# A mixture-of-experts kernel: row codes from one matrix product, two slots joined on TensorE instead of three, and the read-back mixed in after the last items

## The chip, the cores and the metric

The kernel runs on 1 core of one Trainium2 chip. The metric is the device time of one execution in microseconds (us); the kernel before takes 216.29 us (median of 3 runs, 215.59 to 216.37).

## The reference

```python
x = x + ffn(cond(x))                     # x: 32 x 32 tokens, 256 features, float32
def cond(x):                             # a linear layer with one low-rank adapter per batch
    H = einsum('btd,od->bto', x, W)
    return H + einsum('btr,bor->bto', einsum('btd,brd->btr', x, A[idx]), Bm[idx]) * scalings[idx]
def ffn(c):                              # 8 experts, hidden width 704, each token goes to two of them
    weights = softmax_integer(c @ w_gate.T)
    top_w, top_i = top_k(weights, 2); top_w = top_w / top_w.sum(-1)
    out = sum over experts e: combine[:, e] * ((silu(c @ w1[e].T) * (c @ w3[e].T)) @ w2[e].T)
```

## The kernel before

Every token is needed by two experts, so 2048 rows are sorted by expert and packed into 23 slots of 128 rows, each slot of one expert. The kernel first computes the conditioned rows (`c_rows`), the router logits and, on VectorE, each row's position (`pos`). GpSimd then sends rows to their slots in DRAM by indirect DMAs (`send`, two for each of 8 token tiles), and slots 1 to 3 are gathered directly from `cond_rows` (`gather`). For that the kernel needs the token of every slot row (`src_i`), which TensorE makes as a sum of one-hot products, and the row to which each result belongs (`dst_i`, `destinations`), from 24 more such products (`where_rows_belong`). Slot 0 is picked by a product of its own (L1122).

The main loop has 69 items, three for each slot (`s`, `j` = item `i` by 3). In item `i` TensorE does `gate_up(i)`, sometimes `turn_slot` (transposes of the next slot), `turn_hidden(i-1)` and `down(i-2)`. ScalarE does `silu(i)`, `slot_hi` and `hidden_hi(i-1)`; VectorE does `hidden(i)`, `slot_lo`, `hidden_lo(i-1)` and, at `j` = 1, the copy of the finished slot (`slot_out`). Every float32 operand is split into a high and a low part, the weights too: `expert_lo` on VectorE makes the low parts of experts 0 and 1, `low` on GpSimd those of the others. Weights come from the queue of SyncE (`raw_weights`).

The order on each engine is written out by hand and each engine works strictly in it; semaphores are the only ties (`pe.wait_ge(y_out, s)` holds the next slot's `down` until the copy of the last slot is made). The results of the first `SENT` slots go to DRAM by indirect DMAs (`scatter`), are read back in eight DMAs once all of them have landed, scaled (`scale_first`, ScalarE), mixed (`mix`, VectorE) and turned (`turn_sent`, TensorE). The results of the last `DIRECT` slots never leave the core: `join` multiplies them with one-hot matrices (`hot_out`, made by GpSimd, L556) into the four output banks `gu`, two products for each bank and slot. VectorE adds `x` to each bank (L970), and SyncE stores it.

## Time and profile before

| what | value |
|---|---|
| median of 3 runs | 216.29 us |
| the profiled execution | 216.09 us |
| its span in the profile | 214.0 us |
| TensorE busy | 198.9 us, 93% of the span |
| VectorE, ScalarE, GpSimd busy | 50%, 39%, 63% |

The profile shows one execution. Its span is 2.1 us shorter than the time of the same execution, for what lies around it. Times in the rows are us from the start of the span. PE is TensorE, PEld its weight loads, DVE VectorE, ACT ScalarE, POOL GpSimd and SPq the DMA queue of SyncE.

### The profile page before, as it was taken

What the parts mean: (1) busy time and instruction counts of PE and PEld (TensorE: products, weight loads), DVE (VectorE), ACT (ScalarE), POOL (GpSimd) and SP (SyncE); (2) the same over time, 40 slices, a digit from 0 to 9 for tenths busy, and PEclk for the clock granted to TensorE, in tenths of its full rate; (3) what the DMA queues carried; (4) which work ended last, traced back from release to release, by engine and by line L of the source; (5) the groups of instructions that cost most, each with busy time, mean ns of one, the idle gap of its engine ahead of it and who ended that gap; (6) DMA issues with size and microseconds to landing.
All of it is one profiled execution on the core that took longest, in us unless ns stands there. A gap on an engine that the chain in (4) does not pass through costs nothing.

```text
span 214.0 us, 3939 instructions
## 1 busy us (share of the span) xinstructions
PE 198.9 (93%) x1241; PEld 174.3 (81%) x1241; DVE 106.3 (50%) x305; ACT 83.1 (39%) x225; POOL 135.7 (63%) x116
## 2 busy tenths in 40 slices
PE   8899999795899999999999999999999996999990
PEld 6578987683798988989889988989889985888880
DVE  0588899940254543544444542544455533446622
ACT  2476661371783422433323323334224332346500
POOL 8200257877999979999999999930243474295000
PEclk9999999999699999999999999999999999999997
DMA  5999983999499933553464460050012101057005
GB/s 141 408 360 333 335 319 83 324 418 357 152 320 348 348 139 123 176 170 123 138 209 123 121 200 25 28 196 0 28 49 70 58 25 49 28 173 243 3 0 198
DMA packets 23330, 37.12 MB, mean 173 GB/s; under 512 B 2096, under 2 KB 17712, under 8 KB 23184
## 3 DMA queue, kind: packets, MB, share of 16 engines
q1 hardware_dynamic: 19680, 30.15, 42.9%
q0 software_dynamic: 1968, 5.12, 6.7%
q10 hardware_dynamic: 1664, 1.61, 2.3%
q8 instruction: 12, 0.20, 0.4%
q14 instruction: 6, 0.05, 0.1%
HBM read 25.45 MB, written 11.41 MB: 172 GB/s over the span
## 4 chain that ended last, share of the span: by engine, by line
PE 80%; DVE 9%; issue 5%; DMA 3%; ACT 1%; DVEq 0%; SPq 0%
PE gu L1163 26%; PE gu L1172 13%; PE ya L1202 8%; PE ht L1179 7%; PE ya L1203 6%; PE ya L1204 6%; DMA x<-x_t 3%; PE xt L1143 2%; PE gu L1220 2%; PE xt L1122 2%; PE ya L1197 2%; DVE w_all L861 2%; PE ya L1196 1%; DVE raw L970 1%; PE gu L1231 1%
## 5 line engine op out<-in xcount | busy, mean ns | idle before, releaser
L1163 PE MATMUL gu<-w_all,xs_hi 128*128 (+2 forms) x276 | 71.1, 379 | 0.5 <-issue 0.5
L878 DVE TENSOR_TENSOR hid<-gu,sg 128x256 f32<-128x256 f32 x46 | 19.5, 424 | 65.3 <-ACT sg L624 61.6
L1163 PEld LDWEIGHTS gu<-w_all,xs_hi 128*128 128x128 f32 x276 | 47.2, 190 | 4.8 <-issue 0.7
L463 POOL TENSOR_TENSOR w_all<-raw,w_all 128x1024 fp32r<-128x1024 f32 (+2 forms) x15 | 46.9, 3138 | 0.1
L624 ACT ACTIVATE sg<-gu 128x256 f32<-128x256 f32 x46 | 17.6, 384 | 73.4 <-PE gu L1172 69.6
L1202 PE MATMUL ya<-w_all,h_hi 128*128 (+1 forms) x115 | 38.5, 335 | 4.6 <-issue 2.5
L1172 PE MATMUL gu<-w_all,xs_lo 128*128 (+1 forms) x138 | 40.9, 377 | 0.0
L493 POOL DMA_INDIRECT expert_rows<-rows,dst_i x20 | 19.8, 988 | 30.7 <-DVE hid L878 18.5
L1203 PE MATMUL ya<-w_all,h_hi 128*128 (+1 forms) x115 | 32.8, 285 | 0.0
L1204 PE MATMUL ya<-w_all,h_lo 128*128 (+1 forms) x115 | 32.5, 283 | 0.0
L474 POOL DMA_INDIRECT slot_rows<-c_rows,pos_i x16 | 17.3, 1082 | 23.5 <-DVE pos_i L808 18.9
L893 DVE TENSOR_TENSOR h_lo<-ht,h_hi 128x256 fp32r<-128x256 f32 x69 | 28.6, 414 | 2.6 <-issue 1.6
L1172 PEld LDWEIGHTS gu<-w_all,xs_lo 128*128 128x128 f32 x138 | 25.8, 190 | 4.0
L1179 PE MATMUL ht<-ident,hid 128*128 128x128 f32 x138 | 26.4, 273 | 2.5 <-issue 1.6
L567 ACT ACTIVATE h_hi<-ht 128x256 fp32r<-128x256 f32 x69 | 26.8, 388 | 4.0 <-PE ht L1179 4.0
L1202 PEld LDWEIGHTS ya<-w_all,h_hi 128*128 128x128 f32 x115 | 21.8, 189 | 7.0 <-issue 6.0
L1179 PEld LDWEIGHTS ht<-ident,hid 128*128 128x128 f32 x138 | 18.5, 140 | 7.1 <-issue 2.0
L1203 PEld LDWEIGHTS ya<-w_all,h_hi 128*128 128x128 f32 x115 | 21.9, 191 | 0.0
L1204 PEld LDWEIGHTS ya<-w_all,h_lo 128*128 128x128 f32 x115 | 21.9, 190 | 0.0
L522 POOL CAST w_all<-raw 128x1024 fp32r<-128x1024 f32 (+2 forms) x12 | 16.7, 1397 | 1.5 <-DMA raw<-expert_weights 1.4
L628 ACT ACTIVATE sg<-gu 128x128 f32<-128x128 f32 x23 | 6.4, 277 | 27.7 <-PE gu L1172 23.1
L883 DVE TENSOR_TENSOR hid<-gu,sg 128x128 f32<-128x128 f32 x23 | 6.7, 291 | 17.7 <-ACT sg L629 14.1
(194 smaller groups left out, 279.7 us busy)
## 6 DMA issues: line engine op xcount, KB each, us to landing
raw<-expert_weights SPq DMA_DIRECT2D x6, 896.0 KB
raw<-expert_weights SPq DMA_DIRECT2D x6, 640.0 KB
raw<-expert_weights SPq DMA_DIRECT2D x6, 512.0 KB
slot_rows<-zeros SPq DMA_DIRECT2D x1, 2432.0 KB, 16.1
expert_rows<-zeros SPq DMA_DIRECT2D x1, 2048.0 KB, 14.7
rows<-expert_rows SPq DMA_DIRECT2D x8, 256.0 KB, 4.6
rows<-slot_rows SPq DMA_DIRECT2D x1, 1152.0 KB, 9.3
cond_rows<-c_rows ACTq DMA_DIRECT2D x4, 256.0 KB
```

The lines of the kernel that those rows point to most:

```text
L463: return nc.gpsimd.tensor_tensor(lo_part(e, cols), from_raw(e)[:, cols], as_f32(hi_part(e, cols)), ALU.subtract)
L493: nc.gpsimd.indirect_dma_start(out=y_dram[:, :], out_offset=bass.IndirectOffsetOnAxis(ap=dst_i[:, s:s + 1], axis=0), in_=rows[:, s, :], in ...
L567: return nc.scalar.activation(out, in_, ACT.Copy)
L624: nc.scalar.activation(sg[i % 2][:, :].rearrange("p (a b) -> p a b", b=P), bank[:, :].rearrange("p (a k b) -> p a k b", k=2, b=P)[:, :, 0, :],
L878: nc.vector.tensor_tensor(hid[i % HBUFS][:, :].rearrange("p (a b) -> p a b", b=P), bank[:, :].rearrange("p (a k b) -> p a k b", k=2, b=P)[ ...
L893: nc.vector.tensor_tensor(h_lo[i % HBUFS][:, :], ht[i % 2][:, 0:2 * P], as_f32(h_hi[i % HBUFS][:, :]), ALU.subtract).then_inc(h_lo_ready, 1)
L1163: nc.tensor.matmul(out, stay_hi[:, kc * P:(kc + 1) * P], moving(at, part + first + kc * P, n), start=kc == 0 and part == HI_COLS, stop=False)
L1172: last = nc.tensor.matmul(out, stay_lo[:, kc * P:(kc + 1) * P], moving(at, first + kc * P, n), start=False, stop=kc == KC - 1)
L1179: last = nc.tensor.transpose(ht[i % 2][:, q * P:(q + 1) * P], hid[i % HBUFS][:, q * P:(q + 1) * P], ident[:, :])
L1202: nc.tensor.matmul(out, stay_hi, w_l, start=j == q == 0, stop=False)
L1203: nc.tensor.matmul(out, stay_hi, w_h, start=False, stop=False)
L1204: last = nc.tensor.matmul(out, stay_lo, w_h, start=False, stop=False)
```

## The change

Four things change together.

The position code. Before, one product gave the token and 24 more gave "occupied" and "second choice". Now the one-hot product carries one code for each row, token + 1 for a first choice and 1024 more for a second one, 0 for an empty row; VectorE takes `second`, `token` and `src_i` from it (`tokens_of_rows`) and later `dst_i` (`destinations`, now in item 1). `where_rows_belong` and the wait of the first `down` for `dst_ready` go. The code product stands behind the picking of slot 0 on TensorE, not ahead of it. The exponential's polynomial moves from the start of VectorE's program to items 47 to 49, and the picks of slot 0 are made first.

The loads. Expert 2's first piece is asked for right behind expert 1's weights; its second piece waits for the first gather. Three token tiles instead of two are sent ahead of the gathers. `turn_slot` of slots 1 and 4 (`LATE_SLOTS`) stands at `j` = 2, and `c_sent` is two semaphores, so that ScalarE waits for each half of the sends apart.

The last slots. `DIRECT` is 2, so 21 slots are sent, two are joined. The share gathers are two and stand behind scatter 12, not 15.

The end. `scale_first` and `mix` stand in and behind item 69 instead of items 65 to 68, and the last joins stand between the two halves of `turn_sent`.

```diff
-DIRECT = 3
+DIRECT = 2
...
-EARLY_TILES = 2
+EARLY_TILES = 3
+LATE_SLOTS = (1, GATHERED + 1)
+
+FIRST_TILES = 4
...
-SHARES_AT = ITEMS - 19
-SHARES_BEHIND = 15
+SHARES_AT = ITEMS - 22
+SHARE_PARTS = 6
+SHARES_BEHIND = 12
...
+        def turned_at(s):
+            return 2 if s + 1 in LATE_SLOTS else 1
...
+                    if e == STAGED + 1 and k == 1:
+
+                        sp.wait_ge(rows_in[1], 16)
...
             raw_weights(1)
+            raw_weights(2)
 
             sp.wait_ge(xt_done, 1)
-            sp.wait_ge(rows_in[1], 16)
-            raw_weights(2)
             raw_weights(STAGED_LOW)
...
-            nc.gpsimd.iota(token_id[:, :], [[0, TOP], [P, TILES]], base=0, channel_multiplier=1,
+            nc.gpsimd.iota(token_id[:, :], [[TOKENS, TOP], [P, TILES]], base=1, channel_multiplier=1,
...
-                if j == 1 and s + 1 < SLOTS:
+                if j == turned_at(s) and s + 1 < SLOTS:
                     slot_hi(s + 1)
+                if i == ITEMS:
+
+                    scale_first(0)
+                    scale_first(1)
                 if i >= 1:
...
-                        act.wait_ge(c_sent, 16 * CHOICES)
+                    if i > 6:
+
+                        act.wait_ge(c_sent[i - 7], 16 * TOP * FIRST_TILES)
...
-                if ITEMS - 4 <= i < ITEMS:
-                    scale_first(i - (ITEMS - 4))
-
+            scale_first(2)
             direct_hi(SLOTS - 1)
+            scale_first(3)
...
+            chain(nc.vector.scalar_tensor_tensor(first_pos[:, :], by_tile(ranks[:, 0:rank_cols])[:, :, 0], 1.0,
+                                                 picked[:, 0:TILES, 0], ALU.add, ALU.mult))
+            nc.vector.tensor_tensor(picks, row_no[:, :].unsqueeze(1).broadcast_to([P, TILES, P]),
+                                    first_pos[:, :].unsqueeze(2).broadcast_to([P, TILES, P]),
+                                    ALU.is_equal).then_inc(picks_ready, 1)
...
+            def tokens_of_rows():
+
+                dve.wait_ge(src_done, 1)
+                chain(nc.vector.tensor_copy(code[:, :], ht[1][:, 0:SLOTS + 1]))
+                chain(nc.vector.tensor_scalar(second[:, :], code[:, :], TOKENS + 0.5, float(TOKENS),
+                                              ALU.is_gt, ALU.mult))
+                chain(nc.vector.scalar_tensor_tensor(token[:, :], code[:, :], 1.0, second[:, :],
+                                                     ALU.max, ALU.subtract))
+                nc.vector.tensor_scalar(src_i[:, :], token[:, :], 1.0, None, ALU.subtract).then_inc(src_ready, 1)
+
             def destinations():
-                dve.wait_ge(dst_done, 1)
+
+                chain(nc.vector.scalar_tensor_tensor(spare[:, :], code[:, :], 0.0, spare_row[:, :],
+                                                     ALU.is_equal, ALU.mult))
+                nc.vector.scalar_tensor_tensor(dst_i[:, :], code[:, :], 1.0, spare[:, :],
+                                               ALU.subtract, ALU.add).then_inc(dst_ready, 1)
...
             slot_lo(0)
+            tokens_of_rows()
             expert_lo(0, 2)
...
+                if i == 1:
                     destinations()
...
+                if i == ITEMS:
+
+                    dve.wait_ge(weight_ready, 1)
+                    mix(0)
+                    mix(1)
                 if 1 <= i <= ITEMS:
                     hidden_lo(i - 1)
...
-            def where_rows_belong():
-
-                for j in range(CHOICES):
-                    nc.tensor.matmul(ya[:, occ_at:occ_at + SLOTS + 1], hot_r[:, :, j], hot_s[:, :, j],
-                                     start=j == 0, stop=j == CHOICES - 1, skip_group_check=True)
-                for j in range(TILES, CHOICES):
-                    last = nc.tensor.matmul(ya[:, second_at:second_at + SLOTS + 1], hot_r[:, :, j], hot_s[:, :, j],
-                                            start=False, stop=j == CHOICES - 1, skip_group_check=True)
-                last.then_inc(dst_done, 1)
+
+            pe.wait_ge(hot_ready, 1)
+            for j in range(CHOICES):
+                last = nc.tensor.matmul(ht[1][:, 0:SLOTS + 1], hot_r[:, :, j], tok_s[:, :, j],
+                                        start=j == 0, stop=j == CHOICES - 1)
+            last.then_inc(src_done, 1)
...
-                if i == 0:
-                    where_rows_belong()
-                if j == 1 and s + 1 < SLOTS:
+                if j == turned_at(s) and s + 1 < SLOTS:
                     turn_slot(s + 1)
...
                     join(0, 0, first=True)
-                    pe.wait_ge(y_out, SLOTS - 1)
-                    for b in range(KC * HALVES):
-                        join(b, 1)
...
-            for t in range(TILES):
+
+            for t in range(TILES // HALVES):
                 turn_sent(t)
+            pe.wait_ge(y_hi_ready, DIRECT)
+            for b in range(KC):
+                join_part(b, DIRECT - 1, y_hi)
             pe.wait_ge(y_out, SLOTS)
-            for b in range(KC * HALVES):
-                join(b, DIRECT - 1, last=True).then_inc(joined, 1)
+            for b in range(KC):
+                join_part(b, DIRECT - 1, y_lo, last=True).then_inc(joined, 1)
+            for b in range(KC, KC * HALVES):
+                join_part(b, DIRECT - 1, y_hi)
+                join_part(b, DIRECT - 1, y_lo)
+            for t in range(TILES // HALVES, TILES):
+                turn_sent(t)
```

VectorE, the first items: the low parts of experts 0 and 1 (`w_all`), the hidden values (`hid`), `destinations` and `h_lo0`, for which the first `down` waits. Before:

```order
L861 TENSOR_TENSOR w_all<-rows,w_all 128x1792 [waits whi_ready]
L841 SCALAR_TENSOR_TENSOR dst_a<-ya,src_i 128x24 [waits src_ready,dst_done]
L843 SCALAR_TENSOR_TENSOR dst_b<-ya,spare_row 128x24
L845 TENSOR_TENSOR dst_i<-dst_a,dst_b 128x24 [waits dve_step]
L847 TENSOR_TENSOR place<-src_i,dst_b 128x3
L848 TENSOR_SCALAR share_at<-src_i 128x3
L850 TENSOR_SCALAR share_at<-src_i 128x3
L852 ISA share_at<-share_at 128x6 [waits dve_step]
L853 SCALAR_TENSOR_TENSOR share_at<-ya,share_at 128x3 [waits dve_step]
L878 TENSOR_TENSOR hid1<-gu1,sg1 128x256 [waits silu_done]
L870 TENSOR_TENSOR xs_lo1<-xt,xs_hi1 128x256 [waits xs_hi_ready]
L893 TENSOR_TENSOR h_lo0<-ht0,h_hi0 128x256 [waits h_hi_ready]
```

and in the changed kernel, from the row that follows `xs_lo0`:

```order
L846 COPY code<-ht1 128x24 [waits src_done]
L847 TENSOR_SCALAR second<-code 128x24 [waits dve_step]
L849 SCALAR_TENSOR_TENSOR token<-code,second 128x24 [waits dve_step]
L851 TENSOR_SCALAR src_i<-token 128x24 [waits dve_step]
L875 TENSOR_TENSOR w_all<-raw,w_all 128x1280 [waits whi_ready]
L880 TENSOR_TENSOR w_all<-raw,w_all 64x256
L875 TENSOR_TENSOR w_all<-rows,w_all 128x1024 [waits whi_ready]
L892 TENSOR_TENSOR hid0<-gu0,sg0 128x256 [waits silu_done]
L875 TENSOR_TENSOR w_all<-rows,w_all 128x1792 [waits whi_ready]
L892 TENSOR_TENSOR hid1<-gu1,sg1 128x256 [waits silu_done]
L855 SCALAR_TENSOR_TENSOR spare<-code,spare_row 128x24
L857 SCALAR_TENSOR_TENSOR dst_i<-code,spare 128x24 [waits dve_step]
```

The four code operations stand ahead of expert 0's last low part, `hid1` ahead of `destinations` (whose other rows, five, follow, and then `h_lo0`), and `xs_lo1` no longer ahead of `h_lo0`.

ScalarE, the end, where `rows` are the halves read back, `h_hi` the last hidden values and `w_all` the high part of the last joined slot. Before:

```order
L644 ACTIVATE rows<-rows,weight 128x256 [waits y_in2]
L644 ACTIVATE rows<-rows,weight 128x256
L628 ACTIVATE sg0<-gu0 128x128 [waits gu_done]
L629 ACTIVATE sg0<-gu0 128x64
L567 ACTIVATE h_hi1<-ht1 128x256 [waits ht_done]
L644 ACTIVATE rows<-rows,weight 128x256 [waits y_in3]
L644 ACTIVATE rows<-rows,weight 128x256
L567 ACTIVATE h_hi2<-ht0 128x256 [waits ht_done]
L650 ACTIVATE w_all<-ya,share 128x256 [waits share_in,down_done]
```

and in the changed kernel:

```order
L580 ACTIVATE h_hi1<-ht1 128x256 [waits ht_done]
L657 ACTIVATE rows<-rows,weight 128x256 [waits y_in0]
L657 ACTIVATE rows<-rows,weight 128x256
L657 ACTIVATE rows<-rows,weight 128x256 [waits y_in1]
L657 ACTIVATE rows<-rows,weight 128x256
L580 ACTIVATE h_hi2<-ht0 128x256 [waits ht_done]
L657 ACTIVATE rows<-rows,weight 128x256 [waits y_in2]
L657 ACTIVATE rows<-rows,weight 128x256
L663 ACTIVATE w_all<-ya,share 128x256 [waits share_in,down_done]
L657 ACTIVATE rows<-rows,weight 128x256 [waits y_in3]
L657 ACTIVATE rows<-rows,weight 128x256
```

The last hidden value (`h_hi2`) now stands behind two pairs of read-back rows, and the scaling of all eight tiles stands behind item 68.

SyncE's queue, behind the weights of expert 0 and the zeros. Before:

```order
L372 DMA rows<-expert_weights 128x1280
L374 DMA rows<-tail_down_weights 64x256 x2
L372 DMA raw<-expert_weights 128x1024 [waits raw_free0,rows_in1,xt_done]
L372 DMA raw<-expert_weights 128x1792 [waits raw_free1]
L372 DMA raw<-expert_weights 128x1280 [waits w_ready]
L374 DMA raw<-tail_down_weights 64x256 x2
L372 DMA raw_low<-expert_weights 128x1024
L372 DMA raw_low<-expert_weights 128x1792
```

and in the changed kernel:

```order
L385 DMA rows<-expert_weights 128x1280
L387 DMA rows<-tail_down_weights 64x256 x2
L385 DMA raw<-expert_weights 128x1024 [waits raw_free0]
L385 DMA raw<-expert_weights 128x1792 [waits rows_in1,raw_free1]
L385 DMA raw<-expert_weights 128x1280 [waits w_ready]
L387 DMA raw<-tail_down_weights 64x256 x2
L385 DMA raw_low<-expert_weights 128x1024 [waits xt_done]
L385 DMA raw_low<-expert_weights 128x1792
```

Expert 2's first piece lost its wait for the first gather and for slot 0, which expert 2's second piece and expert 3 now carry.

## Rows read from the trace of the kernel before

**Rows 1.** The page: the span, and TensorE's busy time, share and instructions.

```profile
span 214.0 us, 3939 instructions
PE 198.9 (93%) x1241; PEld 174.3 (81%) x1241; DVE 106.3 (50%) x305; ACT 83.1 (39%) x225; POOL 135.7 (63%) x116
```

**Rows 2.** Timeline of VectorE: start us, us, engine, line, operation, [idle before it <- releaser].

```profile
21.23 1.26 DVE L781 SCALAR_TENSOR_TENSOR rt<-rt 128x64 f32<-128x64 f32 x5
...
23.24 0.17 DVE L789 TENSOR_SCALAR filled<-xt 128x8 f32<-128x8 f32 x1
...
27.30 1.22 DVE L819 TENSOR_TENSOR logits<-row_no,first_pos 128x1024 f32<-128x1024 f32 x1
...
32.87 0.42 DVE L870 TENSOR_TENSOR xs_lo<-xt,xs_hi 128x256 fp32r<-128x256 f32 x1 [0.35 <-ACT xs_hi L567]
...
38.34 0.17 DVE L841 SCALAR_TENSOR_TENSOR dst_a<-ya,src_i 128x24 f32<-128x24 f32 x1
...
39.57 0.41 DVE L878 TENSOR_TENSOR hid<-gu,sg 128x256 f32<-128x256 f32 x1
...
40.23 0.41 DVE L893 TENSOR_TENSOR h_lo<-ht,h_hi 128x256 fp32r<-128x256 f32 x1
```

**Rows 3.** Timeline of TensorE at the start.

```profile
27.44 1.22 PE L1113 MATMUL ht<-tok_s,hot_r 128*128 128x24 f16 x16 [0.40 <-DVE tok_s L816]
28.58 3.84 PE L1122 MATMUL xt<-logits,c_rows 128*128 128x128 f32 x32
...
34.40 1.23 PE L1129 MATMUL ya<-hot_s,hot_r 128*128 128x24 f16 x16
...
40.90 0.36 PE L1202 MATMUL ya<-w_all,h_hi 128*128 128x256 f32 x1 [0.42 <-DVE h_lo L893]
```

**Rows 4.** Timeline of GpSimd: its first gather and its last send.

```profile
32.58 0.98 POOL L457 DMA_INDIRECT rows<-cond_rows,src_i  x1 [1.83 <-DMA cond_rows<-c_rows]
...
52.77 0.96 POOL L474 DMA_INDIRECT slot_rows<-c_rows,pos_i  x1 [0.30 <-issue]
```

**Rows 5.** Windows: us, busy PE, PEld, DVE, ACT, POOL, granted clock, DMA share, GB/s.

```profile
46.50:54.60 8.10, 4.39 (x25) 3.31 (x24) 1.92 (x6) 3.25 (x6) 6.55 (x7) 1.00 0.84 336
54.70:58.10 3.40, 3.40 (x13) 2.71 (x12) 0.76 (x2) 2.01 (x4) 3.40 (x2) 0.50 0.42 119
```

**Rows 6.** Timeline in that first stretch, ScalarE and TensorE.

```profile
51.23 0.28 ACT L628 ACTIVATE sg<-gu 128x128 f32<-128x128 f32 x1 [3.12 <-PE gu L1172]
...
54.33 0.38 PE L1202 MATMUL ya<-w_all,h_hi 128*128 x1 [1.70 <-DVE h_lo L893]
```

**Rows 7.** Timeline of TensorE near the end.

```profile
178.69 0.38 PE L1202 MATMUL ya<-w_all,h_hi 128*128 x1 [2.02 <-issue]
```

**Rows 8.** Timeline, VectorE's outputs of slots 19 and 20, one-hot matrices, read-back.

```profile
184.80 0.41 DVE L899 COPY rows<-ya 128x256 f32<-128x256 f32 x1
187.00 8.52 POOL L556 TENSOR_SCALAR w_all<-iota_r,place 128x1024 fp32r<-128x1024 uint16 x3
188.44 3.97 SPq L413 DMA_DIRECT2D rows<-expert_rows  x8
191.74 0.48 DVE L902 SCALAR_TENSOR_TENSOR w_all<-ya,share,w_all 128x256 fp32r<-128x256 f32 x1
```

**Rows 9.** The read-back's DMAs (tile rows, SyncE), issue to landing.

```profile
DMA to landing us min/median/max: 2.8/4.6/5.4
```

**Rows 10.** Timeline of the end: the last hidden value, joins, turns and additions.

```profile
201.84 0.39 ACT L567 ACTIVATE h_hi<-ht 128x256 fp32r<-128x256 f32 x1 [1.24 <-PE ht L1179]
202.35 2.44 PE L1220 MATMUL gu<-w_all 128*128 128x512 f32 x10
...
205.23 1.91 PE L1231 MATMUL gu<-ident,rows 128*128 128x128 f32 x16
...
206.89 2.09 PE L1220 MATMUL gu<-w_all 128*128 128x512 f32 x8
...
207.71 2.48 DVE L970 TENSOR_TENSOR raw<-gu,raw 128x512 f32<-128x512 f32 x4 [1.29 <-PE gu L1220]
```

117 lines of the change are left out of this document (52 added, 65 removed).

## The prediction

> **What bounds the kernel now.** I read the page first: TensorE is busy for 198.9 of 214.0 us [rows 1]. That leaves 15 us of idle time, and a change can win only there, or by taking work off TensorE, or behind its last product. So I went along the chain of waits and then along TensorE's timeline from 30 us to the end, looking for gaps. There are five places. (1) Until the first `down` at 40.90, TensorE follows VectorE: the row says that it waited 0.42 us for `h_lo` [rows 3]. (2) From 46.5 to 54.6 TensorE is busy for only 4.39 of 8.10 us, and behind it the granted clock is 0.50 for 3.4 us, the lower of the two levels, 1.2 GHz [rows 5]. (3) There is 2.02 us of idle time before the `down` at 178.69 [rows 7]. (4) Behind the last `down` come 1.91 us of turns, 2.09 us of joins, and then four additions that end at 207.71 + 2.48 = 210.19 [rows 10]. (5) Otherwise TensorE runs without a gap, and nothing that VectorE, ScalarE or GpSimd do there is on the path.
>
> Place (2) is odd, and the reader should look twice. ScalarE's `silu` at 51.23 waited 3.12 us for a `gate_up` (L1172) [rows 6] whose record on TensorE ends before 48. So the signal was late, not the product. It lies where GpSimd issues sends back to back (the last at 52.77 [rows 4]) while the DMA share is 0.84 [rows 5]. I have no row that names the cause.
>
> **The sum, part by part.** I work from the profiled execution, 216.09 us, which is within 0.2 us of the median of 216.29.
>
> *VectorE's start.* The polynomial (five operations in 1.26 us, all eight from about 21.0 to 23.2) leaves the chain, and the picks (1.22 us) take its place; before, `filled` followed at 23.24 [rows 2]. TensorE's sums that it needs stand ready at about 21.3, so `filled` comes at 21.3 + 0.2 + 1.2 = 22.7, half a microsecond earlier. The one-hots follow, but TensorE is busy with the base products until 27.04 (27.44 less 0.40 idle [rows 3]), so this part alone is worth 0.4.
>
> *The picking of slot 0.* Its 32 products no longer wait behind the 16 code products: they start at 27.04 instead of 28.58 and end near 30.9 instead of 32.4 [rows 3]. The code products follow, 1.2 us, to 32.1. VectorE now waits for them with four chained operations of about 0.2 us (the nearest, `dst_a` and its like, take 0.17 each [rows 2]), until 32.9, and only then goes on to expert 0's last low part, which before began behind `xs_lo` at 32.87 + 0.34 = 33.2 [rows 2]. So of 1.5 us earned on TensorE VectorE passes on about 0.35.
>
> *The first items.* From there VectorE's queue sets the first `down`. Its work up to `h_lo0` loses `xs_lo1` (0.33: `hid` at 39.57 and `h_lo` at 40.23 stand two such operations apart) and one of the eight operations of `destinations`, which take 39.57 − 38.34 = 1.23 us together [rows 2], say 0.05. `h_lo0` comes 0.35 + 0.33 + 0.05 = 0.75 us earlier, and `down` at 40.15 instead of 40.90. The 24 products of `where_rows_belong` (16 of them take 1.23 us [rows 3]) go, but TensorE waits for VectorE there, so they are worth nothing by themselves. Queued behind VectorE's new wait are the low parts of experts 0 and 1; behind GpSimd's wait for `src_i` are the gathers. `src_i` comes at 32.9 instead of 29.8, yet the gathers began only at 32.58, held by the store of `cond_rows` [rows 4], and GpSimd has two more sends to do ahead of them. The first gather starts near 33.7, 1.1 us later, and still lands before TensorE turns slot 1, which now stands at `j` = 2. **Term: −0.75.** If the gather or the store were late by more than 2 us, TensorE would wait for it.
>
> *The sends.* 12 stood behind the gathers, now 10. The last is issued at 52.77 + 1.1 − 2 × 1.27 (0.96 and 0.30 for each [rows 4]) = 51.3, which is 1.4 us earlier, and expert 2's first half megabyte is off the queue by then. If the late signals end when the sends do, TensorE comes out 1.4 us earlier, not 0.75. **Term: −0.65 more**; bounds 0 (the stretch keeps its length) and −5.4, where it goes (8.10 − 4.39 = 3.7 us of idle time, and 3.4 us at half clock, worth 1.7 [rows 5]).
>
> *The middle.* The polynomial's eight operations and the split of the weights stand in items 47 to 52. They take under 0.8 us in an item of 2.3 us, of which VectorE uses half; a hidden value is needed a whole `gate_up` after it is made. 0, and no more than 0.3 if one of them delays. The share gathers go from three to two and stand six items earlier: they were among the back-to-back issues just ahead of the 2.02 us at 178.69 [rows 7]. 0; bounds 0 and −2.0.
>
> *The end.* Slot 20 is now scattered. Its output comes at 191.74, 6.9 us behind slot 19's at 184.80, so the read-back, issued from 188.44 to 191.94, is issued 6.9 us later, from 195.3 [rows 8]. Its second pair of DMAs is issued 1.5 us after the first and lands 4.6 us later (the median; 2.8 to 5.4 [rows 9]): near 201.3. ScalarE stands in item 69 with `scale_first(1)` ahead of the last `h_hi`, which before started at 201.84 [rows 10]; it now starts at 201.3 + 0.9 = 202.2. The last `h_lo` is ready at 203.05 and `down(68)` starts at 203.1. Before, ten join products (2.44 us from 202.35) stood ahead of it and it started at 204.64; now two do. So the last `down` is 1.5 us earlier, although it waits 0.3 us. From it to the end the same 16 turns and 8 joins follow, 3.7 us, to 207.4. The last two banks come together at the very end, and two additions of 0.62 follow where before 2.48 us of four additions began at 207.71: end near 208.6 instead of 210.19 [rows 10]. The `y_hi`, `y_lo` exchange of the last slot hides behind the first eight turns (0.9 us against 1.1), the last `mix` behind the joins of banks 2 and 3. GpSimd's one-hots start behind scatter 20 at 193.8 and, two of 2.84 us (8.52 for three [rows 8]), are ready at 199.5, needed at 200.0. **Term: −1.6**; bounds −0.8 (the second pair lands after 5.4 us) and −1.9.
>
> Sum: 216.09 − 0.75 − 0.65 − 1.6 = **213.1 us**.
>
> A rule that speaks against this sum is in the next part: the clock. The trace agrees with it only behind one gap.
>
> **The rivals.**
>
> *The late signals go.* The first stretch needs something that sends, loads and gathers do together, and the change thins all three. Against it: the sends are still back to back beside a full queue. 216.09 − 0.75 − 5.4 − 1.6 = 208.3; without the second stretch too 206.3. Chance 0.22. Only the second goes (fewer gathers, elsewhere): 213.1 − 2.0 = 211.1. Chance 0.10.
>
> *The gain is eaten.* The first `down` comes no earlier because gather, store or expert 2's early piece delay each other, or the end is held by the read-back (each microsecond that its second pair lands later than 201.3 costs one). Both at their bounds: 216.09 − 0.8 = 215.3, and up to 217. Chance 0.14.
>
> *TensorE's clock falls in the first items (the other side).* With 24 products and a start 0.8 us earlier, TensorE has about 1.9 us of work between 35.0 and 40.15, and waits for VectorE for the rest. The only fall of the clock in the trace follows a stretch with 3.7 us of idle time [rows 5]. If the clock falls here and stays low for 3.4 us, this costs 1.7: 214.8. It is slower than before if it stays low for more than 6 us (3.0 us gained), and by over 0.5% from 8 us on: 217.4. Chance of slower that way or by a longer first stretch 0.12.
> The Trainium skill (TensorE: Matmul & The Clock Gate, "What's actually happening") has the low clock as the default state, released by activity. By that rule the sparser start is a real risk; rows 5 agree with it for the one long gap, and the gaps of 0.9 and 0.4 us before the first `down` left the clock whole.
>
> *The stretches stay as they are*, the forecast: 0.42, with its own range of 212.0 to 215.2.
>
> **How the numbers follow.** The predicted time is that of the likeliest case, 213.1. For 8 in 10 the range reaches down into the case without late signals, to 207.8, and up to 216.2, over most of the case where the gain is eaten. A measurement of this kernel can tell about 0.5%, 1.1 us. Faster than that: 0.42, 0.22 and 0.10 = 0.74; within: 0.15; slower: 0.11.
>
> **What would show it.** In the changed profile: the 32 picking products start near 27.0; `code` on VectorE near 32.1 with some wait; the first gather near 33.7; the first `down` (`ya`) near 40.15 at full clock; the last send near 51.3 and TensorE back at work within 3 us of it, or no gap; two share gathers near item 54; the last read-back issue 6.9 us later against the items; last `down` after a wait under 0.5 us; last addition 3.0 us earlier than 210.19. The prediction is wrong if the signals of TensorE are no longer late, or late elsewhere; if the clock shows 0.50 near 40; or if ScalarE waits for the second pair of the read-back by more than 2 us.

## The result and the profile after

The changed kernel takes 212.16 us (median of 4 executions, 210.32 to 214.19; two more took 209.26 and 209.87), the kernel before 215.94 in the same submission, that is, timed together with it. The ratio is 0.9728, with a 95% interval of 0.9684 to 0.9771: 5.9 us of 215.94. In all that follows the medians are of all executions, while the ratios leave out those in the slower of two states. The profile below is of an execution of 213.79 us with a mean granted clock of 0.98; those of 209.26, 209.87 and 210.32 have 1.00, and none of them was profiled.

Later submissions met other levels, as the median of the kernel before is called here:

| kernel before, median | changed kernel, median | ratio (95%) |
|---|---|---|
| 215.94 | 212.16 | 0.9728 (0.9684 to 0.9771) |
| 209.98 | 206.53 | 0.9829 (0.9773 to 0.9886) |
| 217.88 | 215.09 | 0.9851 (0.9784 to 0.9918) |
| 211.62 | 205.68 | 0.978 (0.949 to 1.007) |

So the change gains 3.2 to 5.9 us by the ratios (2.8 to 5.9 between the medians); the interval of the last row, with two executions of the changed kernel, includes 1. The kernel before against itself, sent once more at the level of 210, gave 1.0115 (1.005 to 1.018): a difference of 1%, about 2 us, between two kernels is weak evidence here, and the profile has to carry it.

The page of the changed kernel: busy time, and TensorE, its granted clock and the DMA share in 40 slices.

```profile
PE 195.0 (92%) x1209; PEld 171.0 (81%) x1209; DVE 106.7 (50%) x307; ACT 83.1 (39%) x224; POOL 134.0 (63%) x115
...
PE   8799997770999999999999999999999999999982
...
PEclk9999999997599999999999999999999999999999
DMA  5999993699499963364265172034011112000845
```

TensorE has 3.9 us less work, yet the span fell only by 2.2, to 211.8. The slice with a 0 is the place: the stretch of [rows 5] was not shortened but is one hole now. Windows of it (columns as in [rows 5]):

```profile
46.40:52.70 6.30, 0.00 (x0) 0.01 (x1) 0.85 (x2) 1.97 (x2) 4.88 (x6) 0.84 1.02 410
52.70:56.60 3.90, 3.90 (x12) 3.32 (x13) 0.82 (x3) 1.68 (x4) 3.90 (x2) 0.50 0.37 137
```

The start, timelines of TensorE, then VectorE, then GpSimd, which answer to [rows 2, 3, 4]:

```profile
31.35 1.17 PE L1185 MATMUL gu<-w_all,xs_hi 128*128 128x512 f32 x4 [0.40 <-issue]
...
35.71 0.44 PE L1201 MATMUL ht<-ident,hid 128*128 128x128 f32 x2 [1.36 <-DVE hid L892]
...
37.92 0.44 PE L1165 MATMUL xt<-ident,rows 128*128 128x128 f32 x2 [0.72 <-DMA rows<-cond_rows,src_i]
...
39.32 0.36 PE L1222 MATMUL ya<-w_all,h_hi 128*128 128x256 f32 x1 [0.75 <-DVE h_lo L907]
```

```profile
22.00 0.16 DVE L802 TENSOR_SCALAR filled<-ht 128x8 f32<-128x8 f32 x1
...
31.62 0.17 DVE L846 COPY code<-ht 128x24 f32<-128x24 f32 x1
...
32.26 0.18 DVE L851 TENSOR_SCALAR src_i<-token 128x24 uint32<-128x24 f32 x1
...
38.76 0.42 DVE L907 TENSOR_TENSOR h_lo<-ht,h_hi 128x256 fp32r<-128x256 f32 x1
```

```profile
34.25 1.93 POOL L470 DMA_INDIRECT rows<-cond_rows,src_i  x1 [0.96 <-issue]
...
51.64 0.96 POOL L487 DMA_INDIRECT slot_rows<-c_rows,pos_i  x1 [0.30 <-issue]
```

The first `down` is 1.58 us earlier than in [rows 3]. ScalarE's copies of the hidden value (`h_hi`) are good milestones, one for each item. The ninth (item 8) starts 1.3 us later than before (the first row is of the changed kernel, the second of the kernel before):

```profile
64.38 0.38 ACT L580 ACTIVATE h_hi<-ht 128x256 fp32r<-128x256 f32 x1
```

```profile
63.06 0.38 ACT L567 ACTIVATE h_hi<-ht 128x256 fp32r<-128x256 f32 x1
```

The gain of the start and 1.3 us more went in the stretch. ScalarE's wait for the sends, which the change splits in two, plays no part in this pair: it comes to the piece of expert 3's weights behind that wait without one in both kernels, at 59.09 before and 60.40 after, when the sends have landed.

```profile
59.09 1.72 ACT L567 ACTIVATE w_all<-raw_low 128x1792 fp32r<-128x1792 f32 x1
```

```profile
60.40 1.71 ACT L580 ACTIVATE w_all<-raw_low 128x1792 fp32r<-128x1792 f32 x1
```

The stop at 178.69 [rows 7] is gone, and gives about 1.5 of it back. The end, timelines of ScalarE, TensorE and VectorE, as in [rows 10]:

```profile
201.65 0.91 ACT L657 ACTIVATE rows<-rows,weight 128x256 f32<-128x256 f32 x2 [1.30 <-DMA rows<-expert_rows]
202.46 0.36 ACT L580 ACTIVATE h_hi<-ht 128x256 fp32r<-128x256 f32 x1
```

```profile
203.55 0.38 PE L1222 MATMUL ya<-w_all,h_hi 128*128 x1 [0.70 <-DVE h_lo L907]
...
207.00 1.03 PE L1252 MATMUL gu<-ident,rows 128*128 128x128 f32 x8
```

```profile
206.16 1.28 DVE L1002 TENSOR_TENSOR raw<-gu,raw 128x512 f32<-128x512 f32 x2
207.96 1.29 DVE L1002 TENSOR_TENSOR raw<-gu,raw 128x512 f32<-128x512 f32 x2 [0.52 <-PE gu L1252]
```

The last addition ends at 209.25 instead of 210.19, and the span 2.55 us behind it, not 3.81. That last difference was in no term of the sum.

### The profile page after: what moved, and what is told of

It is laid out like the page before. It is cut to its first block, busy times and chain, and to the rows that moved or that the text cites. A ratio compares the mean times of both kernels' runs of the same rounds, so it can differ in the third digit from the quotient of the medians.

```text
span 211.8 us, 3877 instructions
## 1 busy us (share of the span) xinstructions
PE 195.0 (92%) x1209; PEld 171.0 (81%) x1209; DVE 106.7 (50%) x307; ACT 83.1 (39%) x224; POOL 134.0 (63%) x115
## 4 chain that ended last, share of the span: by engine, by line
PE 75%; DVE 9%; DMA 7%; issue 5%; ACT 1%; SPq 1%; DVEq 0%; POOLq 0%
PE gu L1185 26%; PE gu L1194 13%; PE ya L1222 7%; PE ht L1201 6%; PE ya L1223 6%; PE ya L1224 6%; DMA x<-x_t 3%; DVE w_all L875 3%; DMA rows<-expert_rows 2%; PE xt L1165 2%; PE ya L1217 1%; PE ya L1216 1%; DMA expert_rows<-rows,dst_i 1%; PE gu L1067 1%; PE gu L1239 1%
## 5 line engine op out<-in xcount | busy, mean ns | idle before, releaser
L506 POOL DMA_INDIRECT expert_rows<-rows,dst_i x21 | 20.7, 986 | 36.6 <-DVE hid L892 17.7
L1222 PEld LDWEIGHTS ya<-w_all,h_hi 128*128 128x128 f32 x115 | 22.1, 192 | 10.4 <-issue 9.4
L1223 PEld LDWEIGHTS ya<-w_all,h_hi 128*128 128x128 f32 x115 | 22.3, 194 | 0.0
```

Source lines behind the costliest of these rows:

```text
L506: nc.gpsimd.indirect_dma_start(out=y_dram[:, :], out_offset=bass.IndirectOffsetOnAxis(ap=dst_i[:, s:s + 1], axis=0), in_=rows[:, s, :], in ...
L1222: nc.tensor.matmul(out, stay_hi, w_l, start=j == q == 0, stop=False)
L1223: nc.tensor.matmul(out, stay_hi, w_h, start=False, stop=False)
```

## The experiments

The theory after this profile: (1) the start is worth 1 to 1.5 us; (2) the sends' stretch has two stops, signals that come late, and ScalarE's single wait for all sends in item 7, which the split `c_sent` takes away; (3) the end is worth about 2 us. The main rival to (2) is that the split wait is worth nothing. A signal is called late where an engine still waits for a product or a copy that the profile has as done. Unless a run says otherwise, a kernel stands beside the kernel before at 209.9 to 210.

**The same kernels again.**

> The changed kernel once more, nothing edited. Its first four times fall in two groups, 210.3 and 210.5 against 213.8 and 214.2, and the profile shown is of the second group: TensorE idle for 6.40 us before the `down` at 52.70. Theory A (signals of TensorE and of the DMAs come late while sends and loads fill the DMA queues, in some executions and not in others): a trace of the first group has no gap over 1 us there, and the others' median lies near 210.4, a ratio of 0.972. Theory B (the gap is a fixed wait of this order of instructions): every trace has the gap, and the two groups differ elsewhere.

> The kernel before once more, nothing edited; ratio 1.00. Its trace had 3.7 us of idle time between 46.5 and 54.6 and 2.0 us before 178.7. Theory A: another execution has these gaps shorter, longer or elsewhere, and since its times lie within 0.8 us of each other, something else takes their place when they are gone (ScalarE's wait for all 16 sends, which landed at 55.0). Theory B: the same gaps in the same places.

Changed: 206.53 us (205.12 to 207.78). The level was lower, and no signal was late: between 46 and 58 us TensorE is busy for 11.94 of 12 us, although the DMA share is as full as above.

```profile
46.00:52.00 6.00, 6.00 (x41) 5.31 (x40) 2.19 (x7) 5.14 (x11) 4.48 (x6) 1.00 1.02 404
52.00:58.00 6.00, 5.94 (x34) 4.74 (x32) 2.01 (x8) 4.40 (x9) 5.98 (x3) 1.00 0.56 196
```

Before: 212.3 us (211.65 to 213.44). Here too no signal was late, but another stop stood in its place (ScalarE, then TensorE, then windows):

```profile
56.55 1.70 ACT L567 ACTIVATE w_all<-raw_low 128x1792 fp32r<-128x1792 f32 x1 [3.63 <-DMA slot_rows<-c_rows,pos_i]
```

```profile
59.11 0.69 PE L1179 MATMUL ht<-ident,hid 128*128 128x128 f32 x2 [2.68 <-DVE hid L885]
```

```profile
59.10:61.50 2.40, 2.39 (x10) 2.17 (x11) 1.04 (x3) 1.71 (x4) 2.40 (x2) 0.50 1.00 336
```

ScalarE stands 3.63 us at its piece of expert 3's weights until all 16 sends have landed; `silu` and `hidden_hi` are queued behind it, and TensorE waits 2.68 us and then runs at half clock. In the first profiles this stop was hidden: TensorE was late anyway.

**The split wait, from both sides.**

```diff
-                    if i > 6:
-                        act.wait_ge(c_sent[i - 7], 16 * TOP * FIRST_TILES)
+                    if i == 7:
+                        act.wait_ge(c_sent[0], 16 * TOP * FIRST_TILES)
+                        act.wait_ge(c_sent[1], 16 * TOP * FIRST_TILES)
```

> The changed kernel, but ScalarE waits in item 7 for all 16 sends, as the kernel before does, instead of for one half in item 7 and for the other in item 8. If the split wait is where the gain beyond the forecast comes from: ScalarE stands in item 7 (near 49.5) until the last send has landed (near 54), and the time rises by 2 to 4 us over the changed kernel where the signals are on time (near 213.5, ratio near 0.985). Rival (the gain beyond the forecast is the missing late signals alone): no change, ratio near 0.972.

209.47 us (206.75 to 211.0, 10 runs) against 206.53, ratio 0.9947 (0.991 to 0.999) against 0.9829: the single wait costs 2.9 us by the medians, 2.5 by the ratios, and the stop is that of the kernel before (ScalarE waits 3.56):

```profile
57.75 0.44 PE L1201 MATMUL ht<-ident,hid 128*128 128x128 f32 x2 [2.59 <-DVE hid L899]
```

The other way round, the kernel before with the split alone:

```diff
-        c_sent = sem("c_sent")
+        c_sent = [sem(f"c_sent{i}") for i in range(2)]
...
-                    if i == 7:
-                        act.wait_ge(c_sent, 16 * CHOICES)
+                    if i > 6:
+                        act.wait_ge(c_sent[i - 7], 16 * CHOICES // 2)
```

> The kernel before with one part of the change alone: the semaphore of the sends is two, one for each half, and ScalarE waits for the first half in item 7 and for the second in item 8. Theory A (the single wait for all 16 sends is what stalls TensorE near 57 to 59 us when nothing signals late; 2.7 us before turn_hidden in the kernel before): 2.5 to 3.5 us faster than the kernel before when both are free of late signals, and the gap before that turn_hidden under 0.5 us. Theory B (the wait only shares a stall that the late signals make anyway; the gain in the changed kernel came from its shorter start): within 0.8 us of the kernel before, the gap moves to another instruction of the same stretch. If late signals come in this execution, both theories give a gap of 3 to 6 us in front of ScalarE's silu and a difference near 0, which then says nothing.

208.58 us (207.76 to 211.3), ratio 0.9964 (0.993 to 0.9998) to the kernel before beside it. That is 0.8 us, not the 2.5 to 3.5 expected; from the 212.3 us above, where the wait was long, it is 3.7. No wait stands before that `turn_hidden`, and none over 0.2 us between 42 us and the end. So the stop is the single wait's, and the split is worth 0.8 us in the kernel before and 2.5 to 2.9 in the changed one. Why it differs is not shown: no execution of the kernel before near 209.5 us was profiled. The run also gives the cleanest pair of profiles: this one and that of the changed kernel without late signals (spans 205.8 and 203.6). Their first `down`, before and after:

```profile
40.42 0.36 PE L1202 MATMUL ya<-w_all,h_hi 128*128 128x256 f32 x1 [0.42 <-DVE h_lo L893]
```

```profile
39.45 0.35 PE L1222 MATMUL ya<-w_all,h_hi 128*128 128x256 f32 x1 [0.66 <-DVE h_lo L907]
```

**Expert 2's early piece.**

```diff
             raw_weights(1)
-            raw_weights(2)
...
             sp.wait_ge(xt_done, 1)
+            sp.wait_ge(rows_in[1], 16)
+            raw_weights(2)
```

> The changed kernel, but expert 2's first piece is asked for only behind slot 0's picking and the first gather, as before. If the early piece thins the queue enough to matter: sends, loads and late signals last longer, 1 to 3 us slower (ratio 0.977 to 0.986). Rival (the early piece rather held the store of `cond_rows` and so the first gather, which started at 34.25 and not 33.7): the first gather starts near 33.3, TensorE's 0.72 us wait for slot 1 goes, same time or up to 0.5 us faster (ratio 0.970 to 0.972).

206.73 us (205.51 to 208.35) against 206.53, first `down` at 39.51 against 39.45. The wait for the gathered rows goes, one for `hid` of 0.55 takes its place. The early piece is worth nothing that shows.

**The products taken out, and three joined slots.**

```diff
+                if i == 0:
+                    for n in range(CHOICES + CHOICES - TILES):
+                        nc.tensor.matmul(ya[:, 256:256 + SLOTS + 1], ...)
```

> The changed kernel with 24 products of the size of the 24 that were taken out, at their old place behind the first gate_up, into columns that nothing reads. I put the taken products at nothing, since TensorE waits for VectorE until the first down. That gives 0 (within 0.5 us) and the first down at the same time, with shorter gaps ahead of it. The rival: they sit on the chain from gate_up to hidden, and the kernel is 1.0 to 1.8 us slower, with the first down later by as much.

205.3 us (204.67 to 206.31); the first `down` at 39.55, with TensorE's wait ahead of `turn_hidden` filled. The 24 products cost nothing, as predicted.

```diff
-DIRECT = 2
+DIRECT = 3
...
                     join(0, 0, first=True)
+                    pe.wait_ge(y_out, SLOTS - 1)
+                    for b in range(KC * HALVES):
+                        join(b, 1)
```

> The changed kernel with three last slots joined on TensorE again instead of two; its read-back, mixing and order of the last joins stay. Eight more join products stand ahead of the last down and their wait for the copy of the slot before. By my sum the end as a whole was worth 1.6 us, with bounds 0.8 and 1.9; the profile of the changed kernel shows 0.8. If the joined slot is what the end gained by, this kernel is 1.4 to 1.9 us slower than the changed one (206.5 when nothing is late). If the end gained by the later mixing instead (the rival), it is within 0.5 us of it.

208.1 us (206.53 to 208.88, 10 runs), 1.6 slower by the median, 0.8 by the span (204.4 against 203.6). The joined slot is worth 0.8 to 1.6 us, no more than the difference between two medians of one kernel, but the profile shows it too; the span behind the last addition stays at 2.5 us.

**The work on the chains that end last.**

```diff
-                if i == 1:
-                    destinations()
...
                     mix(0)
-                    mix(1)
                 if 1 <= i <= ITEMS:
                     hidden_lo(i - 1)
+                if i == ITEMS:
+                    mix(1)
+                if i == 3:
+                    destinations()
```

(and `scale_first(1)` behind `hidden_hi` in item 69)

> The changed kernel with two pieces of work moved off chains that end last: VectorE's two operations of destinations go from item 1 to item 3, behind its low part of the hidden value, and in item 69 the second scaling (ScalarE) and the second mix (VectorE) go behind the last high and low part of the hidden value. If VectorE's queue sets the first down, that comes 0.9 us earlier; if the last down waits for ScalarE's scaling and not for the read-back, its wait of 0.70 us falls to near 0. Both: 1.0 to 1.6 us faster than the changed kernel. If instead another wait (hid, the gathered rows of slot 1) takes their place, the gain is under 0.5 us.

205.85 us (205.3 to 206.22) against 206.53, ratio 0.9826 against 0.9829: of the 1.0 to 1.6 us expected nothing is clear of the noise. The first `down` came at 38.63, 0.82 earlier, and the last one without a wait, both as expected. But slot 2 was not there yet, and the start's gain was lost at once: a wait for DMA, `rows<-cond_rows,src_i`, of 0.99 us at 44.38. The gathered rows are what is late next.

**At a level of 215.3: the order at the end, the order at the start, both late edits.**

```diff
-            for t in range(TILES // HALVES):
+            for t in range(TILES):
                 turn_sent(t)
...
+            for b in range(KC * HALVES):
+                join_part(b, DIRECT - 1, y_hi)
+                join_part(b, DIRECT - 1, y_lo, last=True).then_inc(joined, 1)
```

> The changed kernel with the order of the last products as before: all eight turn_sent, then the joins of all four banks, so that four additions and four stores come together at the end. In the profile of the changed kernel the last store is issued 2.2 us before the end of the span, in that of the kernel before 3.5 us, though both issue four stores of the same size; before, they come within 2.1 us, after the change within 2.7 us and in pairs. Theory A: bunched stores land later, and the new order is worth 1.3 us behind the last addition and 0.6 to 0.9 us ahead of it: 1.9 to 2.2 us slower than the changed kernel (206.5 when nothing is late), 3.4 us or more from the last issue to the end. Theory B (the stores' time doesn't depend on the order, the difference is chance): 0.6 to 0.9 us slower, 2.2 us from the last issue to the end.

213.79 us (210.92 to 215.98), ratio 0.9872. The unchanged kernel was not timed in this submission, so the times of this and the next two runs can't be set against it; the profiles must do. The bunched stores are not slow: the span ends 2.7 us behind the last addition. From the start of the last `down` to the end of the span it takes 8.97 us, 0.4 to 0.8 more than in four profiles of the changed kernel. Theory A falls. What the 3.8 us of the kernel before were, the DMA queues say. Of its span from 211 us to the end:

```profile
q1 hardware_dynamic: 223, 0.39, 35.4%
q14 instruction: 1, 0.01, 0.6%
```

One of the six 8 KB blocks of instructions is fetched among the last stores, and the last of the 16 engines' shares of the last store lands 1.04 us behind the other 15 (213.59, 212.55). The same holds in all four profiles of the kernel before and of its variant (1.04 to 1.08 us), and in none of the 16 of the changed one and its variants, where the block is fetched about 4 us before the end and the last share lands with the others. For the four stores, issue to landing, the kernel before, the changed kernel and this variant:

```profile
DMA to landing us min/median/max: 2.1/2.2/3.4
```

```profile
DMA to landing us min/median/max: 2.0/2.2/2.4
```

```profile
DMA to landing us min/median/max: 2.2/2.3/2.3
```

Where the block falls was in nobody's plan, so this gain is luck. That the block delays the share is likely, not shown: I did not move it by itself.

```diff
+            pe.wait_ge(hot_ready, 1)
+            for j in range(CHOICES):
+                last = nc.tensor.matmul(ht[1][:, 0:SLOTS + 1], ...)
             pe.wait_ge(picks_ready, 1)
...
+            tokens_of_rows()
             slot_lo(0)
-            tokens_of_rows()
```

> The changed kernel with the 16 code products ahead of the picking of slot 0 on TensorE again, and VectorE's four operations on the code ahead of the low part of slot 0, as before the change. I gave the order of the two 0.35 of the 0.75 us of the start. My sum: slot 0 is picked 1.2 us later, VectorE's wait for the code goes, and the first down comes 0.3 to 0.5 us later; TensorE's wait of 0.8 us for the gathered rows of slot 1 shrinks but is taken by VectorE's queue. Time: 0.2 to 0.5 us slower than the changed kernel. The rival (the gather sets the first items, so that the earlier code pays): first down 0.3 to 0.6 us earlier and the kernel faster by that.

212.18 us (211.27 to 213.42), ratio 0.9839. The first `down` came at 39.19, not later than in the changed kernel (39.32 to 39.68 in four profiles). The first gather still started at 34.86, held by a send of 1.84 us ahead of it. By this profile the order of code and picking is worth nothing either way, against my 0.35.

> The changed kernel with the two edits of the last batch together: destinations in item 3 and the last scaling and mix behind the last high and low part, and expert 2's first piece asked for only when slot 1's rows are in. With the first edit alone the first down came 0.8 us earlier, and a new wait of 0.99 us for the gathered rows of slot 2 took it back. If expert 2's early piece delays the gathers, that wait falls to 0.3 us or less and the kernel is 0.5 to 0.8 us faster than with the first edit alone (205.9): 205.2 or a little under. If GpSimd's three issues themselves set the gathers, the wait stays near 1.0 us and the time at 205.9.

(The edits that moved `destinations`, the last scaling and the last mix, and expert 2's first piece behind the first gather, together.) 211.1 us (208.71 to 213.4), ratio 0.9764. No wait for slot 2's rows this time, but TensorE ran at half clock in its first items, so the two can't be told apart by it:

```profile
38.45:41.85 3.40, 3.25 (x13) 3.06 (x14) 2.96 (x7) 0.77 (x2) 2.79 (x3) 0.50 0.55 170
```

A wait of 1.36 us ends at 36.37 and one of 0.74 us at 38.60; the changed kernel has the same two, and its clock stayed whole. So the fall of the clock that the prediction feared does occur, in one profile of the 16 of the changed kernel and its variants.

> The kernel before again, unchanged. Most of its times on this chip are near 209.6 and some near 213. The profile shown so far of this chip is of 211.65, with a wait of 2.7 us for all 16 sends and the clock at half level behind it. If this execution is near 209.6, theory A (the single wait is worth what the sends' end decides) expects the same wait with 1.0 to 1.5 us and no fall of the clock; the rival (another place differs) expects that wait unchanged at 2.7 us and 2 us less elsewhere.

218.93 us: with late signals again, 2.81 and 1.70 us of idle time before 54.63 and 56.77. Neither expectation could be tested.

**What makes signals late.** At a level of 217.9:

```diff
-            raw_weights(STAGED_LOW)
...
             slot_rows(0)
+            raw_weights(STAGED_LOW)
...
-                if 6 <= i < 9:
+                if 9 <= i < 12:
```

> The changed kernel again, unchanged, to stand beside the two below. On a chip on which the kernel before takes near 210 it shows no gap between 42 and 56 us and is 3.4 us faster; on one on which the kernel before takes near 215.5, I expect late signals again: TensorE idle for 3 to 7 us between 46 and 54, and 4.5 to 6 us faster than the kernel before.

> The changed kernel with expert 3's weights (2.9 MB) asked for only when all sends have landed, behind the rows of slots 4 and up, and ScalarE's high parts of them in items 9 to 11 instead of 6 to 8, where its wait for the sends stands now too. Theory A (signals are late where sends and loads fill the queues together): the DMA share between 48 and 54 falls, TensorE's idle time there falls from 3 to 7 us to under 1 us, and on such a chip the kernel is 3 to 6 us faster than the changed one. Theory B (the sends alone do it, or something outside the kernel): the gap stays at 3 us or more and the time within 1 us. On a chip without late signals both expect the wait of 0.9 us for the second half of the sends to go, and 0.3 to 0.7 us.

> The last edit together with that which moves destinations to item 3 and the last scaling and mix behind the last high and low part. Without late signals: first down 0.8 us earlier, the wait for slot 2's gathered rows (0.99 us) stays or shrinks by up to 0.7 since expert 3's load no longer lies beside it, the last down without a wait: 1.0 to 2.0 us faster than the changed kernel. With late signals: as the run before, and 0.8 us more.

The changed kernel, unedited, took 215.09 us, with one hole of 5.60 us before 52.17 and half clock behind it:

```profile
46.57:52.17 5.60, 0.00 (x1) 0.01 (x1) 1.27 (x3) 2.30 (x3) 4.11 (x5) 0.81 1.02 404
52.17:56.00 3.83, 3.83 (x12) 3.09 (x12) 0.45 (x3) 0.88 (x4) 3.80 (x3) 0.50 0.56 217
```

With expert 3's weights held back it took 212.91 (210.63 to 218.63), and with the other edits 212.82 (210.58 to 215.22), ratio 0.9795. Windows of the first of the two:

```profile
46.00:49.00 3.00, 2.89 (x17) 2.23 (x15) 0.27 (x1) 0.96 (x1) 2.39 (x3) 1.00 0.52 192
49.00:52.40 3.40, 0.47 (x3) 0.23 (x3) 0.91 (x3) 1.40 (x4) 2.49 (x4) 1.00 0.25 87
```

The DMA share is 0.25, and TensorE still stands for 3.0 us in all (1.31 and 1.73; 3.9 in the other). Full queues are not needed. The stop is 1.7 to 2.6 us shorter than with the loads, and the time 2.2 us by the medians: neither theory's number, and with one profile of each no more than a hint that the loads lengthen it. In the same profile VectorE's copy of a finished slot is 2.04 us late just behind five indirect DMAs that GpSimd issued back to back, with the DMA share at 0.2:

```profile
163.80 0.97 POOL L561 DMA_INDIRECT share<-shares,share_at  x1 [0.32 <-issue]
165.08 0.97 POOL L561 DMA_INDIRECT share<-shares,share_at  x1 [0.30 <-issue]
166.35 1.01 POOL L505 DMA_INDIRECT expert_rows<-rows,dst_i  x1 [0.30 <-issue]
167.66 0.99 POOL L505 DMA_INDIRECT expert_rows<-rows,dst_i  x1 [0.30 <-issue]
```

```profile
169.72 0.42 DVE L912 COPY rows<-ya 128x256 f32<-128x256 f32 x1 [2.04 <-remote]
```

That suggested a last pair: take the string of sends away, or break it.

```diff
-            for t in range(EARLY_TILES, TILES):
-                send(t)
```

```diff
             for t in range(EARLY_TILES, TILES):
                 send(t)
+                if t in (4, 5):
+                    low_of(2, t - 4)
```

> The changed kernel unchanged, as the reference for the two below on the same chip. If the kernel before is near 210 here, no signal is late and the three runs tell nothing of the cause; if it is 214 or more, TensorE stands idle for 3 to 7 us between 46 and 54 us.

> The changed kernel without the ten sends behind the gathers: the rows of the last five token tiles are not sent (this part of the computation is left out), and the rows of slots 4 and up are read back as soon as the six early sends have landed and two experts are ready. The loads stay. Theory C (a long string of back-to-back indirect DMAs on GpSimd makes signals late): the string ends with the gathers near 40, no idle time over 1 us between 42 and 56, 4 to 7 us faster than the changed kernel on a chip with late signals. Theory A (the loads fill the queues): DMA share is still near 1.0 from 40 to 50, and gaps of 2 us or more stay. Theory B (something outside the kernel): a gap somewhere there too.

> The changed kernel with two pieces of GpSimd's work on expert 2's low parts (2.4 and 4.1 us) put between the sends, behind tile 4 and behind tile 5: the string of 13 indirect DMAs becomes pieces of 7, 2 and 4, and the last send is issued 6 to 8 us later, so slot 4's rows come late and TensorE waits 2 to 6 us for them near 58. Theory C in its strong form (a string of more than about five is what it takes): no late signal between 46 and 54, and a wait of TensorE for the DMA of slot_rows instead. If the number of sends matters and not that they stand back to back, the late signals go on until the last send, near 60.

205.68, 204.72 and 212.61 us, the kernel before at 211.62. No signal was late in the reference, so the pair says nothing of the cause. It prices the sends: sent 6.6 us later (the last issue at 58.58 instead of 51.99) they cost 6.9 us. Without the late ones 1.0 us is gained, from two executions of each, which is within the noise. ScalarE shows where the 6.9 us go:

```profile
61.01 1.27 ACT L585 ACTIVATE w_all<-raw_low 128x1280 fp32r<-128x1280 f32 x1 [6.15 <-DMA slot_rows<-c_rows,pos_i]
```

Set side by side, the profiles say one thing more. Late signals stand in all nine profiles of the three submissions at levels of 215.3 to 217.9, whatever the kernel, and in none of the eleven of the three at 209.9 to 211.6, though nine of these have the whole string of sends. So in every profile on record whether they come goes with the submission; the kernel decides at most where and for how long.

## Why the prediction came out as it did

The measured time lies in the range (207.8 to 216.2), but by the ratio the change gained 5.9 us, about twice the 3.0 of the sum. That 213.1 is within 0.9 us of the median of 212.16 is luck: none of the six executions took between 210.6 and 213.7, and errors of both signs stand in the terms.

- **The step that failed: the sends**, −0.65, that is, the assumption that the stretch of late signals stays as it was and ends 1.4 us earlier. "If the late signals end when the sends do, TensorE comes out 1.4 us earlier": in the profile they did end with them (TensorE is back at 52.70, the last send is issued until 52.60), but it came out having done less, and the term was a loss of 2.9 us, from the start's gain to the hidden value of item 8. Nor did the stretch stay in the executions on which the ratio rests, 209.3 to 210.5 us. Three of these four have a granted clock of 1.00, so the piece at half clock, 3.9 us in the profile and worth 2 us, is missing; and since the clock fell behind every such hole that was profiled, the hole is likely gone too. The rival "the late signals go", 208.3 with a chance of 0.22, comes nearest. But in the profiles late signals follow the submission and not the kernel. Why the changed kernel escaped the hole in some executions of a submission in which the kernel before took 215.3 us or more each time stays open: none of them was profiled.
- **The split wait** has no term at all. I described the second semaphore among the changes and gave it no price: in [rows 6] ScalarE waits for `gate_up`, and with late signals it comes to the sends' wait when that is long over. Where signals are on time the runs price it at 0.8 to 2.9 us.
- **The start**, −0.75: first `down` −1.58 in the first pair of profiles, −0.97 in the clean pair (40.42 and 39.45). Too small because the start was earlier than I had it: the base products end sooner, the picking starts at 26.22 and not at 27.04, `src_i` is there at 32.26 and not at 32.9, without a wait of VectorE for the code, and `destinations` took 0.91 us instead of 1.18. But it is not kept: in the clean pair the difference is 0.20 us at the item that starts near 61, behind ScalarE's wait of 0.88 us for the second half of the sends. "It still lands before TensorE turns slot 1" was wrong by 0.72 us, hidden behind VectorE. The products of `where_rows_belong` were worth nothing, as said, and so was expert 2's early piece. I had worried for the clock here: waits of 1.36, 0.72 and 0.75 us left it at 1.00 in this profile, but in one variant the same waits, 1.36 and 0.74 us, came with 0.50 for 3.4 us from 38.45, so the worry was sound. By the Trainium skill (TensorE: Matmul & The Clock Gate, "What's actually happening") the low clock is the default that activity releases; the trace agrees behind the long holes, 0.50 behind 6.30, 5.60 and 2.68 us, and with the short waits of the start in one profile of 16.
- **The middle**, 0 with a bound of −2.0: the stop at 178.69 did go in the first pair. One of its kind came back at 170 in a variant, so this belongs to the late signals, not to the change.
- **The end**, −1.6: −2.1 in the profile, from the last `gate_up` group at the start of item 68 (197.78 and 197.65) to the end of the span. Only 0.8 of it is what the sum meant, up to the end of the last addition, half of the term. The mechanism was right: the last `down` waited for the read-back as predicted, but 0.70 us, not 0.3, since ScalarE got its data at 201.65 for the 201.3 forecast. So the last addition ended 0.94 us earlier than before on the clock of the span, not 1.6. The other 1.26 lies behind it and had no term; it goes with the block of instructions that no longer falls among the last stores. The Trainium skill (Perfetto Trace Analysis, "DMA Instruction — HWDGE (DVE, Sync)") says that the semaphore of a DMA is updated only when the write before it is confirmed, and that this can take surprisingly long, above all where the target is HBM. No run here separates that wait; both kernels store to the same place, and the trace shows one engine late in the kernel before, not all.
- Clean pair, as a balance: start −0.97, of which 0.77 is lost by 61 us; the end of the last addition −0.85 in all; behind it −1.3; sum −2.2 of 205.8. With the 0.8 us of the split that is 3.0 us, beside 3.6 by the ratio at that level (0.9829 of 209.98). The forecast of 3.0 us is near this too, and that is luck as well: of its three terms, the start is nearly all lost again, the sends' has nothing to work on, and the end has 0.85 of its 1.6. The split and the end of the stores, which had no term, fill the gap.

Open: what makes TensorE's signals late. Shown is that it comes and goes between submissions of one kernel, goes with 8 us of span in one pair (211.6 and 203.6 for the same program: 5.6 us hole, 1.9 for half clock behind it), doesn't need full DMA queues, and stood each time in or just behind a string of 5 to 15 indirect DMAs. Whether the string is the cause is not shown: strings of the same length are in the profiles without it. Nor is it shown that late signals are all of the difference between the levels: at 215.3 the kernel before has executions of 214.2 to 214.6 us at a granted clock of 1.00, where at 210 such ones take 209.4 to 209.5, and no profile of the former exists.

## What to carry to other kernels

Price every wait that a change splits or moves, also where the profile shows another reason for the idle time: a wait for several things hides all but the last, and what it hides may be as long. When the bound of a stretch comes and goes between executions, take the profile of both levels before trusting either. And a gain on one chain is kept only until the next one that is late: here 0.8 us at the first `down` lasted 6 us, until slot 2's gather.

## What the hardware showed that I had not expected

- The same program runs at levels almost 4% apart (209.98 to 217.88 us for the kernel before); in the one pair of profiles of the same program at both levels nearly all of the difference lies in one stretch of 10 us.
- In such profiles ScalarE and VectorE wait 2 to 6 us for products of TensorE that are recorded as done. Nine profiles have it and eleven not, by submission and not by kernel.
- In the four profiles in which an 8 KB block of instructions is fetched among the last stores, one share of the last store lands 1.04 to 1.08 us behind the others, and the span ends 3.8 us behind the last addition, against 2.5 to 2.8 in six of those without.
- The same waits of about 1.4 and 0.7 us left the clock whole in most profiles and came with half clock for 3.4 us in one.
